# Last batch by query halves, its tails' blocks at a distance of 11 steps, a fourth q/k slot, and another order of the ternary weights in batch 0

## What is computed

```
q, k, v = x @ Wq.T + bq, x @ Wk.T + bk, x @ Wv.T + bv      # 16 heads of 16
q, k = rope(q) * 16**-0.5, rope(k)
x = layernorm(x + softmax(q @ k.T) @ v @ Wo.T + bo)
W1t, W2t = ternary(W1), ternary(W2)                       # values -1, 0, 1
out = layernorm(x + relu(x @ W1t.T + b1) @ W2t.T + b2)    # hidden size 1024
```

## Time and profile before

| | us |
|---|---|
| median of three runs | 3300.49 |
| profiled execution | 3303.37 |
| its span | 3301.6 |
| TensorE busy | 3248.1 (98%) |
| VectorE busy | 2990.3 (91%) |
| ScalarE busy | 2532.8 (77%) |
| POOL busy | 2149.4 (65%) |
| last batch begins, its attention ends | 3040.6, 3235.7 |

### The profile page before, as it was taken

The page is one execution under the profiler, slowest core; times in us unless marked ns, Lnnn a source line. Parts: engine busy times, 40 slices in busy tenths (PEclk is TensorE's granted clock), DMA queues, the critical chain, the costliest instruction groups (busy, mean ns, idle before and its releaser), DMA issues. The chain is left out here.

```text
span 3301.6 us, 82481 instructions
## 1 busy us (share of the span) xinstructions
PE 3248.1 (98%) x31190; PEld 1786.8 (54%) x31190; DVE 2990.3 (91%) x5721; ACT 2532.8 (77%) x4971; POOL 2149.4 (65%) x2440
## 2 busy tenths in 40 slices
PE   6999999999999999999999999999999999999997
PEld 4444555555555555555555555555555555555546
DVE  7889999999999999999999999999999999999965
ACT  3777777777777777777777777777777777777773
POOL 2575766766766766766766766766766766754444
PEclk7999999999999999999999999999999999999999
DMA  8444354454354354354454354354354354354211
GB/s 215 108 99 105 92 116 103 98 116 109 91 116 108 93 116 107 93 116 104 97 116 109 92 116 107 93 116 108 92 116 105 95 116 107 93 110 86 57 42 54
DMA packets 312557, 341.27 MB, mean 103 GB/s; under 512 B 77280, under 2 KB 260448, under 8 KB 312160
## 3 DMA queue, kind: packets, MB, share of 16 engines
q1 hardware_dynamic: 311584, 335.20, 44.4%
q10 hardware_dynamic: 576, 0.79, 0.2%
HBM read 195.37 MB, written 140.51 MB: 102 GB/s over the span
## 5 line engine op out<-in xcount | busy, mean ns | idle before, releaser
L1074 DVE TENSOR_REDUCE mxp<-ms 128x1 f32<-128x512 f32 x4064 | 2617.6, 683 | 232.2 <-PE ms L749 186.5
L900 ACT ACTIVATE prob<-sc 128x512 f32<-128x512 f32 x4096 | 2225.5, 597 | 634.3 <-PE sc L760 607.3
L760 PE MATMUL sc<-qa,ka 50*128 50x512 f32 x4096 | 1543.3, 445 | 4.3 <-DMA qa<-maxima 3.4
L749 PE MATMUL ms<-ka,qa 48*128 48x512 f32 x4064 | 1537.3, 446 | 2.9 <-DVE mxp L1292 2.2
L760 PEld LDWEIGHTS sc<-qa,ka 50*128 50x128 f32 x4096 | 688.9, 185 | 1067.9 <-ACT prob L900 918.8
L777 PE MATMUL ob<-prob,v_sb 128*17 128x512 f32 (+1 forms) x8656 | 1094.2, 577 | 2.7 <-ACT at_st L907 2.4
L749 PEld LDWEIGHTS ms<-ka,qa 48*128 48x128 f32 x4064 | 684.1, 185 | 10.0 <-DVE mxp L1074 3.9
L1405 POOL TENSOR_TENSOR ve<-mv,eps_sb 128x2 f32<-128x2 f32 x119 | 23.4, 197 | 492.8 <-DVE mv L1101 492.8
L1426 POOL TENSOR_TENSOR hid_r<-hid,hid_r 128x512 fp32r<-128x512 f32 x240 | 308.7, 1286 | 19.2
L777 PEld LDWEIGHTS ob<-prob,v_sb 128*17 128x17 f32 x8656 | 143.7, 95 | 273.5 <-issue 273.2
L597 PEld LDWEIGHTS job<-h_t,w_sb 64*128 64x128 f32 x3840 | 261.0, 186 | 23.7 <-issue 0.6
(11 more groups left out here) (157 smaller groups left out, 2843.3 us busy)
## 6 DMA issues: line engine op xcount, KB each, us to landing
qk_parts<-parts SPq DMA_DIRECT2D x122, 512.0 KB, 4.3
ka<-qk_parts SPq DMA_DIRECT2D x378, 128.0 KB, 4.7
qa<-qk_parts SPq DMA_DIRECT2D x378, 128.0 KB, 7.4
attention<-at_st SPq DMA_DIRECT2D x128, 256.0 KB, 3.0
v_ones<-v_st SPq DMA_DIRECT2D x64, 272.0 KB, 2.4
v_sb<-v_ones SPq DMA_DIRECT2D x64, 272.0 KB, 8.4
xn<-x SPq DMA_DIRECT2D x64, 256.0 KB, 4.8
ao<-attention SPq DMA_DIRECT2D x128, 128.0 KB
```

The costliest lines, as they stand in the source:

```text
L749: nc.tensor.matmul(ms[upto(b, g, NS1, at) % MS_BANKS][:, :], operand(qa, b, g, j, ROWS)[:, qt * P:(qt + 1) * P], operand(ka, b, g, j, ROWS ...
L760: nc.tensor.matmul(sc[upto(b, g, HG * STEPS, n) % SC_BANKS][:, :], operand(ka, b, g, j, ROWS + MROWS)[:, tt * P:(tt + 1) * P], operand(qa, ...
L900: nc.scalar.activation(prob[st_ % 2][:, j, :], sc[upto(b, g, HG * STEPS, n) % SC_BANKS][:, :], ACT.Exp).then_inc(s["exp_done"], 1)
L1074: nc.vector.reduce_max(mxp[(b * G + g) % 2][:, kh, j * TT + qt:j * TT + qt + 1], ms[upto(b, g, NS1, at) % MS_BANKS][:, :], AX.X).then_inc( ...
```

## The change

**Last batch.** Its attention runs over query halves first: steps 0 to 31 take the queries 0 to 511 of all four head groups, steps 32 to 63 the rest (`half_at`). All four groups' q and k must then be there at once, so there is a fourth slot (index `RING`). The third group is loaded into it in the last unit of batch 14, behind `move_maxima` for half 1; the fourth at the start of the last batch. Values are loaded anew for each half.

The tails of batch 14 (k = 0 to 3) and the first two of batch 15 (k = 4, 5) start every 11 steps in the last batch. A block spans 17 steps and overlaps with the next: its g0 to g3 stand in steps 2 to 5 of the next block, where that one has no job. f0 stands one step behind t4, not two. The work of POOL, VectorE and SP for a tail is given by the step r within the block. Behind attention there remain f2 to g3 of tail 1, and tails 2 and 3 with the former functions.

**Batch 0.** In unit 2 three pieces of W1 stand where four stood; the fourth and two pieces of W2 come at the end of the unit; the other two pieces of W2 come behind `add_products` in unit 3. There SP moves the maxima before it waits for the eight pieces.

Both need two more memsets at the start (rows of ones in the fourth slot).

```diff
+LAST_PERIOD = 11
+LAST_JOBS = {0: "t3a", 1: "t3b", 6: "t4", 7: "f0", 8: "f1", 9: "f2", 10: "f3", 13: "g0", 14: "g1", 15: "g2", 16: "g3"}
+LAST_FIRST_NORM = {(1, 1): "sum 0", (1, 2): "sum 1", (2, 1): "stats 0", (2, 3): "stats 1", (3, 0): "moments 0"}
+LAST_SECOND_NORM = {(16, 1): "sum 0", (16, 2): "sum 1", (17, 1): "stats 0", (17, 3): "stats 1", (18, 0): "moments 0"}
+LAST_RECIP_AT = (3, 3)
+def half_at(b, g, qh):
+    at = QH * g + qh
+    return (at % G, at // G) if b == B - 1 else (g, qh)
+def last_tails_at(step):
+    return [(k, step - LAST_PERIOD * k) for k in range(G + 2) if step >= LAST_PERIOD * k]
...
 # SP, unit
                 if (b, g) == (0, G - 1):
+                    move_maxima(b, g, 1)
                     sp.wait_ge(s["ternary_done"], 2 * TERNARY_PIECES)
                 if prepared(b, g)[0] >= 0:
                     tail_in(*prepared(b, g))
-                move_maxima(b, g, 1)
+                if (b, g) != (0, G - 1):
+                    move_maxima(b, g, 1)
+                if (b, g) == (B - 2, G - 1):
+                    load_rows(B - 1, 2, slice(0, S), qk_loaded[slot_of(B - 1, 2)])
                 if len(proj) > 1:
                     proj_out(*proj[0])
                 for at in projected_next(b, g):
                     proj_in(*at)
                 store_attention(b, g, 0)
                 if prepared(b, g)[0] >= 0:
                     attention_in(*prepared(b, g))
...
 # SP, last batch
+                for st_ in range(G * STEPS):
...
+                    if st_ % TT == 5 and st_ < (G * QH - 1) * TT:
+                        move_maxima(b, after // QH, after % QH)
+                    for k, r in last_tails_at(st_):
+                        if r == 1:
+                            tail_in(*last_tail(k + 1))
+                            if k <= G:
+                                load_attention(*last_tail(k + 1))
+                        elif r == 4 and k <= G:
+                            store_reciprocals(*last_tail(k + 1))
+                        elif r == 5 and k <= G:
+                            load_reciprocals(*last_tail(k + 1))
+                        elif r == 9:
+                            tail_out(*last_tail(k - 1))
+                store_attention(b, G - 1, 1)
+                tail_out(b, 0)
+                attention_in(b, 2)
...
 # TensorE, behind the last batch
-            frees = tail_job(end, 0, "t4", 0, [("t6_taken", upto(end, 0, TL, 0))], True)
+            frees = run(("tail", (end, 1), "f2"), frees)
             weigh(end, G - 1, STEPS - 1)
+            for name in ("f3", "g0", "g1", "g2", "g3"):
+                frees = run(("tail", (end, 1), name), frees)
...
+            frees = whole(tail_job, end, 2, "t3", frees, True)
+            frees = tail_job(end, 2, "t4", 0, frees, True)
             f_free = [[], []]
-            for g in range(G):
+            for g in range(2, G):
...
 # POOL, last batch
+                    if st_ % TT == 4 and st_ < (G * QH - 1) * TT:
+                        split_maxima(b, after // QH, after % QH)
+                    for k, r in last_tails_at(st_):
+                        at = last_tail(k)
+                        if r == 3:
+                            finish_first_norm(*at)
+                        elif r == 4:
+                            sum_h1(*at)
+                        elif r == 5:
+                            sum_x(*last_tail(k + 1))
+                        elif r == 6:
+                            split_first_norm(*at)
+                        elif r == 7 and k > 0:
+                            finish_second_norm(*last_tail(k - 1))
+                        elif r == 8:
+                            split_hidden(*at, 0)
+                            split_hidden(*at, 1)
+                        elif r == 9:
+                            if k <= G:
+                                normalise(*last_tail(k + 1))
+                        elif r == 11:
+                            split_hidden(*at, 2)
+                            split_hidden(*at, 3)
...
 # POOL, unit
                 for at in proj[:1]:
                     add_products(pool, nc.gpsimd, *at)
                 if (b, g) == (0, 2):
-                    for piece in range(TERNARY_PIECES):
+                    for piece in range(TERNARY_PIECES - 1):
                         ternary(0, piece)
+                elif (b, g) == (0, G - 1):
+                    for piece in range(2, TERNARY_PIECES):
+                        ternary(1, piece)
...
                 if (b, g) == (0, 2):
-                    for piece in range(TERNARY_PIECES):
-                        ternary(1, piece)
+                    ternary(0, TERNARY_PIECES - 1)
+                    ternary(1, 0)
+                    ternary(1, 1)
```

More of the change, by code:

```diff
@@ L277, in build @@
         s = {n: sem(n) for n in names}
-        qk_loaded = [sem(f"qk_loaded{i}") for i in range(RING)]
+        qk_loaded = [sem(f"qk_loaded{i}") for i in range(RING + 1)]
         v_loaded = [sem(f"v_loaded{i}") for i in range(2)]
@@ L313, in banks_of @@
                 return ms[0], ob
-            if end and name == "t3 0":
-                return ms[0], ms[1]
             return job
@@ L474, in tail_out, with unit @@
                              ).then_inc(s["out_stored"], 16)
-            def unit(b, g, tail, last, first, tail_before):
+            def unit(b, g, tail, first, tail_before):
                 proj = projected(b, g)
@@ L499, in unit, with batch, last_batch @@
                     attention_in(*prepared(b, g))
-                if not (last and g == G - 1):
-                    move_maxima(b + (g + 1) // G, (g + 1) % G, 0)
+                move_maxima(b + (g + 1) // G, (g + 1) % G, 0)
                 for at in proj[-1:]:
                     proj_out(*at)
-            def batch(b, tail=True, last=False, first=False, tail_before=True):
+            def batch(b, tail=True, first=False, tail_before=True):
                 for g in range(G):
-                    unit(b, g, tail, last, first, tail_before)
+                    unit(b, g, tail, first, tail_before)
+            def last_batch():
+                b = B - 1
+                sp.wait_ge(s["s2_ready"], upto(b, 0, HG * STEPS, 0))
+                load_rows(b, G - 1, slice(0, S), qk_loaded[slot_of(b, G - 1)])
+                for st_ in range(G * STEPS):
+                    g, qh = st_ // STEPS, st_ // TT % QH
+                    if st_ % TT == 1:
+                        before = QH * g + qh - 1
+                        store_attention(b + before // (QH * G), before // QH % G, before % QH)
+                        if before + 2 < QH * G:
+                            load_v(b, (before + 2) // QH, before % QH)
+                    if st_ % TT == 5 and st_ < (G * QH - 1) * TT:
+                        after = QH * g + qh + 1
+                        move_maxima(b, after // QH, after % QH)
[13 more added lines that the diff above has]
+                attention_in(b, 2)
+                tail_in(b, 3)
+                attention_in(b, 3)
+                for g in range(1, G):
+                    tail_out(b, g)
             first_in(0)
@@ L565, in _ @@
             batch(B - 2)
-            batch(B - 1, last=True)
-            tail_in(B - 1, 1)
-            attention_in(B - 1, 1)
-            store_attention(B - 1, G - 1, 1)
-            tail_out(B - 2, G - 1)
-            for g in range(2, G):
-                tail_in(B - 1, g)
-                attention_in(B - 1, g)
-            for g in range(G):
-                tail_out(B - 1, g)
+            last_batch()
             sp.wait_ge(s["out_stored"], 16 * B * G)
@@ L1057, in _ @@
             take_outputs(B - 1, G - 1, 1)
-            take_last_norm(0)
-            for g in range(G):
+            finish(("tail", (B - 1, 1), "f3"))
+            finish_rest(("tail", (B - 1, 1), "f3"))
+            take_last_norm(2)
+            for g in range(2, G):
                 for n in range(FT // 2):
@@ L1341, in _ @@
             batch(B - 2)
[L1342 to L1350 removed]
+            last_batch()
+            for p in range(2):
+                take_hidden(B - 1, 1, 2 + p, job[1][:, p * TQ:(p + 1) * TQ])
+            invert(B - 1, 2)
+            last_second_sums(1, job)
+            last_second_moments(B - 1, 1)
+            last_first_sums(2)
+            last_first_moments(2)
+            last_second_norm(B - 1, 1)
+            last_first_norm(2)
+            invert(B - 1, 3)
+            take_last_low(2)
+            for g in range(2, G):
+                if g > 2:
+                    last_second_sums(g - 1, banks_of("g", True))
                 take_last_hidden(g, 0)
[L1352 to L1353 removed]
                 take_last_hidden(g, 1)
@@ L1494, in ternary, with last_batch, unit @@
                                         ).then_inc(s["ternary_done"], 1)
-            def unit(b, g, tail, tail_before, last):
+            def last_batch():
+                b = B - 1
+                finish_second_norm(b - 2, G - 1)
```

(12 more changed lines are left out.)

171 lines of the change are left out of this document (99 added, 72 removed).

## The result

The changed kernel takes 3319.7 us (median, 3319.5 to 3322.3) against 3301.9 for the kernel before in the same rounds. The ratio is 1.0056, 95% interval 1.0044 to 1.0068: slower by 17.8 us, where 7.5 had been forecast, and just outside the range (3294 to 3318). The profiled execution took 3320.0 with a span of 3318.2, against 3301.6 before.

The account below looks back on a forecast made before the run. TensorE, busy 98% of the span, was taken as the bound. Terms +4.0 + 1.9 + 9.1 - 8.5 = +6.5, with about one more for VectorE bursts +7.5, gave 3308 us (own range 3303 to 3312; overall 3294 to 3318).

Parts of the forecast that it names:

- Batch 0: Batch 0's last units: maxima wait and half clock go (-6.0), den wait (+7.5) and half clock (+2.5) come; +4.0 us.
- Fourth slot: Last unit of batch 14: attention store waits behind twelve q/k loads, den lands late, TensorE loses 1.9 us.
- steps of the last batch: Last batch's attention: 60 steps with a job, 4 without, small extras; 195.2 us against 195.1 before.
- The job that waits: Last batch: f0 waits for low h1, held on POOL behind VectorE's addition for the tail before; +9.0 us in sum.
- End: Behind the last exponential: 54.9 us against 65.9, less an allowance for half clock; -8.5 us, range -6 to -11.
- one period of 14.4: End: 14.4 us from tail 2's first f0 to tail 3's, within the 54.9 us sum.
- The other term: End: a half-clock stretch around t3, with TensorE idle before and behind it, put at 2.5 us.
- (a): Last batch: f0 does not wait, since the addition is early enough or slack absorbs the stall; 3299 us, chance 0.15.
- (b): Batch 0: only the den wait is hidden, -10 us; 3298 us, chance 0.09.
- (c): Both the f0 waits and batch 0's den wait are hidden; 3289 us, faster, chance 0.10.
- (e): Batch 0: the change does not free the maxima, +6 us; 3314 us, chance 0.06.
- (d): Last batch: f0 waits bring down the clock, 3.3 us a time, +10 to +20; 3318 to 3328 us, chance 0.10.

Follow-up runs that it names:

- 3: Changed kernel, but in batch 0's last unit SP stores attention and reads den and the attention result before waiting for the ternary pieces: 3311.6 us, ratio 1.0036.
- 1: Changed kernel with batch 0's former order of ternary pieces and SP waits: 3316.4 us, ratio 1.0048.
- 7: Kernel before plus only the batch 0 part of the change, unmended: 3306.8 us, ratio 1.0016.
- 10: Kernel before plus only the batch 0 part, with den and the attention result read before SP waits for the pieces: 3294.7 us, ratio 0.9976.
- 5: Changed kernel with the fourth slot's six q loads in batch 14 issued behind the next maxima, not before the attention store: 3318.8 us, ratio 1.0049.
- 4: Changed kernel with POOL doing h1's rounding and low part before the h1b and x sums in the last batch: 3319.8 us, ratio 1.0057.
- 2: Changed kernel with tail 1's x, den and attention loads issued before the fourth group's twelve loads: 3313.7 us, ratio 1.0041.
- 13: Kernel 11 with the last batch's low part of h1 on VectorE, and ScalarE writing the rounded h1: 3290.7 us, ratio 0.9961.
- 14: Kernel 13 with the low part of h1 one reduction earlier on VectorE: 3288.1 us, ratio 0.9967.
- 9: Changed kernel with VectorE's reciprocal for the last tail moved ahead, behind tail 1's moments: 3319.8 us, ratio 1.0056.
- 8: Changed kernel with the mends of 2, 3, 4, 5 and 6 together: 3298.8 us, ratio 0.9990.
- 11: Kernel 8 plus the earlier reciprocal of 9: 3293.4 us, ratio 0.9975.
- 12: Kernel 11 without the filling matmuls at the end: 3298.3 us, ratio 0.9989.
- 6: Changed kernel plus matmuls that nobody reads in TensorE's idle times at the end: 3321.4 us, ratio 1.0055.

## Why the prediction was wrong

- **Batch 0** (+4.0, measured +4.3, of which 3.7 in the units 2 and 3): right in both halves. The maxima wait and its half clock went, worth 6.0 as forecast (99.1 against 93.1 in 3). The wait for den came (7.9 forecast, 7.80 measured; TensorE 7.5 and 7.13) with a half-clock stretch of 10.2 us, together 9.7 against 10.0. Shown by 1, 3 and 7. The wait for den costs nothing to remove: den is read in front of the wait for the pieces (3, 10).
- **Fourth slot** (+1.9, measured +2.0): right; the store behind the twelve loads landed after 6.1 us, shown by 5. The Trainium skill, "DMA: Bandwidth & Descriptors", section "Queues, rings and completion order", says that a DMA engine consumes a queue's descriptors in ring order, though a later one may finish before an earlier one. The 6.1, against 2.0 with six of the loads moved behind the store, agrees with the ring order. The clock was luck: it stayed full behind TensorE's 1.45 us here, but fell for 3.4 us behind the same wait (1.4 to 1.7 us) in 1, 3 and 4, whose batch 14 took 197.5 to 197.8.
- **The failed step, steps of the last batch** ("60 x 3.08 + 4 x 2.66 ... 195.2"). It priced the fourth slot for batch 14 only. The fourth *group*, twelve more loads, goes out at the very start of the last batch, and the reciprocal, moved from step 10 to step 3, meets it. I had priced exactly this pattern a unit earlier and did not apply it here. Cost: 16.23 - 10.72 = 5.5 us, of which TensorE stood for 2.63 (VectorE for 2.96) and the rest goes with the 6.8 us at half clock. Shown by 2 and, from the other side, by 5 (17.99 with more loads in front). With it the sum closes: 195.2 + 5.5 + 7.9 for the next item = 208.6, against 209.3.
- **The job that waits** (+9.0, measured 7.9): right in mechanism and size, block by block: 1.45 four times against 1.38, 1.49, 1.37 and, in block 5, where VectorE has no reductions left, 0.77; 2.35 against 2.17; 0.8 against 0.68. Experiment 4 took off what POOL's two sums cost, 13 and 14 the rest but for 1.4 us in six steps.
- **End** (-8.5, measured -4.3). Here too a step failed: the term "one period of 14.4", which measured 19.8. It was taken over from the kernel before, where the reciprocal of the next tail stands in front of the second norm of the tail before (4.8 us before the first f0), and in the later periods in front of both norms (7.7 and 6.6 us before f0). In the changed kernel VectorE does it behind both (3279.39, 2.1 us before f0), so the attention product and t3 of tail 3 come late. Moving it took the period from 19.8 to 15.4 without the filling (9) and from 17.2 to 13.2 with it (8 against 11, though 8 had a half-clock stretch of 3.4 us in it as well): about 4 us. The other term is half clock, mis-sized only: 31 us in four stretches, the last 3.4 without TensorE work. It cost 3.4 to 4.6 (9 and 12 against 11), where I had allowed 2.5. With both mended the end takes 54.0, against 54.9 in my sum without half clock. In that sum the terms up to tail 2's f0 add to 23.1, not 23.6; it came at 24.0 in 11, so the closeness of the total is in part luck.
- **Rivals.** (a) is refuted by the six waits, (b) and (c) by the wait for den, (e) by the trace of the turn. (d), that the f0 waits bring down the clock, did not happen in the profiled execution of the changed kernel, but it did in 2 (two f0 steps), 3, 4 and 12 (one each). Its price there was 1.4 to 2.4 us a time, not 3.3. The measured 3319.7 lies within (d)'s 3318 to 3328, but by other causes. Its premise, that an idle of 1.30 us leaves the clock full, held in the kernel before by chance: behind that same wait it fell in 6 and 7. The steps that failed were none of my rivals.
- **The value of the idea.** With batch 0 mended alike, the old last batch gives 3294.7 (10) and the new one 3293.4 (11): no difference that can be told. But 11 has the filling of the end and 10 has not. Without it the new one takes 3298.3 (12), so of the new order alone no gain is shown. With the f0 waits gone as well (14: 197.6 + 54.2 = 251.8, against 191.0 + 64.3 = 255.3 in 10) the trace shows 3.5 us for the new order, the filling and the low part on VectorE together. The old last batch with a filled end was not run, so that rival is open. In kernel 10 the old order had full clock in the last unit, which it had not in the profiled execution of before.

## What to carry to other kernels

When a step is moved earlier, ask at its new place what the same queue has issued in the last ten microseconds; a load of 16 KB took 2.2 us in the median, 8.3 behind the twelve loads, and 10.6 with six more in front. When a period is taken over from the kernel before, check that every engine's program still has the same order inside it. And where there are several small waits behind which the clock falls in one execution and not in the next, judge a mend by its stage first and mend them together: one at a time some showed nothing in the median (4, 5, 6, 9), all together took the changed kernel from 3319.7 to 3293.4 (11).

## What the runs showed of the hardware

- The granted clock fell in every trace that had a TensorE wait of 2.6 to 4.1 us for den early in the last batch (seven kernels), of 6.7 to 7.1 us for den in batch 0 (seven kernels), or of 2.6 and 2.7 us for the maxima (the kernel before and 1). It fell within the wait or less than 1 us behind it; in the changed kernel 1.7 us into the 2.63 us before 3063.17, and 2.5 us into the 7.13 us before 261.05.
- Behind shorter waits it fell in some traces and not in others: behind 1.31 us in batch 0 (in 6 and 7 alone), 1.4 to 1.8 in batch 14 (in 1, 3 and 4 of seven kernels), and 0.5 to 1.9 in front of f0 (in 2, 3, 4 and 12). With the same code and a wait of 1.5 us it fell in 12 and not in 8 and 11.
- After the program's first 85 us and before its last few it stayed down for 3.4, 6.8, 10.2, 17.1 or 20.5 us.
- Stretches at half clock appear without such a wait as well. In the profiled execution of the kernel before TensorE was busy for all 10.3 us from 3201.4 on, at half clock, in the unit without maxima, and idle for no more than 0.21 us at a time in the 15 us before. Kernel 7 had such a stretch at the same place; in kernel 10 the clock stayed full there.
- With the filling, 42 matmuls that nobody reads, the clock stayed full through the idle times between the last exponential and tail 3's f0 (1.00 in the third window of 11), where about 15 us at half clock stood without it (12).
